# Two chained recurrent layers of 1024 steps: a third tile of layer 0 split for 88 columns, and the matmuls, rests and copies of a step put in another order

## What is computed

```python
def _L0_cond_ref(x, h0, Wx, Wh, b):
    xW = jnp.einsum('ntd,dh->nth', x, Wx) + b
    def step(h_prev, xw_t):
        h_next = jnp.tanh(h_prev @ Wh + xw_t)
        return (h_next, h_next)
    _, hs = jax.lax.scan(step, h0, jnp.swapaxes(xW, 0, 1))
    return jnp.swapaxes(hs, 0, 1)
...
    x = x + _L0_cond_ref(x, cond_1024, L0_cond_Wx, L0_cond_Wh, L0_cond_b)
    x = x + _L1_cond_ref(x, cond_1024, L1_cond_Wx, L1_cond_Wh, L1_cond_b)
```

## Time and profile before

| what | value |
|---|---|
| median of 3 runs | 2058.94 us (2058.87 to 2059.46) |
| the profiled execution | 2059.2 us, its span 2057.4 us |
| TensorE matmuls busy | 2046.2 us (99%) |
| TensorE weight loads busy | 1952.7 us (95%) |
| VectorE busy | 1837.9 us (89%) |
| ScalarE busy | 1539.9 us (75%) |
| GpSimd busy | 444.0 us (22%) |
| granted TensorE clock | full in all of 40 slices |

### The profile page before, as it was taken

How to read it: one execution, slowest core, us unless ns; L and a number is a source line. 1 busy time by engine, 2 the same in 40 slices (tenths; PEclk the granted TensorE clock), 3 DMA queues, 4 the chain that set the end, 5 groups by cost and what they waited for, 6 DMA issues and landing times.

```text
span 2057.4 us, 224159 instructions
## 1 busy us (share of the span) xinstructions
PE 2046.2 (99%) x98384; PEld 1952.7 (95%) x98384; DVE 1837.9 (89%) x12254; ACT 1539.9 (75%) x7426; POOL 444.0 (22%) x2054
## 2 busy tenths in 40 slices
PE   8999999999999999999999999999999999999999
PEld 7999999999999999999999999999999999999998
DVE  5999999999999999999999999999999999999997
ACT  5777777777777777777777777777777777777776
POOL 3222222222222222222222222222222222222221
PEclk9999999999999999999999999999999999999999
DMA  3000000000000000000000000000000000000000
GB/s 106 28 24 28 24 27 25 26 25 26 26 25 26 25 27 24 28 24 28 24 28 24 28 24 28 24 28 24 28 24 28 24 28 24 28 24 27 25 26 18
DMA packets 111995, 56.59 MB, mean 28 GB/s; under 512 B 12432, under 2 KB 111008, under 8 KB 111520
## 3 DMA queue, kind: packets, MB, share of 16 engines
q1 hardware_dynamic: 111168, 53.53, 9.0%
q10 hardware_dynamic: 576, 1.18, 0.2%
q0 software_dynamic: 32, 0.02, 0.0%
HBM read 37.90 MB, written 16.78 MB: 27 GB/s over the span
## 4 chain that ended last, share of the span: by engine, by line
PE 99%; DMA 1%; issue 0%; DVE 0%; ACT 0%; ACTq 0%; SPq 0%
PE ps_rec L303 44%; PE ps_rec L324 33%; PE ps_xw L279 22%; DMA wx<-wx_in 0%; DMA wh<-wh_in 0%; PE ps_rec L376 0%; DVE zt L541 0%; ACT h L445 0%; SPq L255 0%; ACTq L498 0%; ACTq L497 0%; DVE x_out L581 0%; DVE z L550 0%; SPq L254 0%
## 5 line engine op out<-in xcount | busy, mean ns | idle before, releaser
L303 PE MATMUL ps_rec<-wh,h 128*32 128x128 f32 x33024 | 1271.8, 273 | 4.1 <-ACT h L445 2.7
L445 ACT ACTIVATE h<-z 128x16 f32<-128x16 f32 x4066 | 709.2, 217 | 481.7 <-DVE z L550 475.4
L324 PE MATMUL ps_rec<-wh_part,h 128*32 128x128 bf16 x48792 | 1047.4, 219 | 1.5 <-issue 1.5
L303 PEld LDWEIGHTS ps_rec<-wh,h 128*32 128x32 f32 x33024 | 832.5, 109 | 79.6 <-ACT h L445 9.2
L324 PEld LDWEIGHTS ps_rec<-wh_part,h 128*32 128x32 bf16 x48792 | 890.1, 97 | 15.4 <-issue 1.9
L541 DVE STREAM_TRANSPOSE zt<-ps_rec 128x64 f32<-128x64 f32 x4096 | 778.8, 228 | 94.0 <-PE ps_rec L303 14.2
L214 POOL TENSOR_TENSOR h<-h 128x16 f32<-128x16 f32 x2032 | 430.1, 212 | 1589.4 <-DVE h L214 1589.4
L434 ACT ACTIVATE ps_rec<-xw,mask 128x128 f32<-128x128 f32 x2040 | 731.9, 359 | 9.5 <-issue 1.0
L550 DVE TENSOR_REDUCE z<-zt 128x16 f32<-128x48 f32 x4066 | 650.6, 199 | 0.9
L214 DVE TENSOR_TENSOR h<-h 128x16 f32<-128x16 f32 x2034 | 357.3, 176 | 110.7 <-ACT h L445 2.8
L279 PE MATMUL ps_xw<-wx,x_pe 128*32 128x128 f32 x8248 | 409.9, 273 | 0.5 <-issue 0.5
(11 more groups left out here) (23 smaller groups left out, 22.3 us busy)
## 6 DMA issues: line engine op xcount, KB each, us to landing
x_pe<-x_t SPq DMA_DIRECT2D x256, 64.0 KB, 1.9
x_dve<-x_t SPq DMA_DIRECT2D x256, 64.0 KB, 2.0
out_t<-x_out SPq DMA_DIRECT2D x256, 64.0 KB, 1.7
wh<-wh_in SPq DMA_DIRECT2D x1, 1024.0 KB, 5.2
wx<-wx_in SPq DMA_DIRECT2D x1, 1024.0 KB, 8.2
wx<-wx_in ACTq DMA_DIRECT2D x1, 512.0 KB, 5.0
wx<-wx_in SPq DMA_DIRECT2D x1, 512.0 KB, 4.8
wh<-wh_in SPq DMA_DIRECT2D x1, 512.0 KB, 7.9
```

The costliest lines, as they stand in the source:

```text
L303: mm = pe.matmul(rows(ps_rec[l][n % 2], g), h_step(l, n - 1)[:, k, :], wh[l][:, k, g * P:(g + 1) * P], start=False, stop=k == KC - 1 and n ...
L324: mm = pe.matmul(ps_rec[l][n % 2][32 * g:32 * g + 32, cols], h_bits(l, n - 1)[:, k, :], wh_part[l][:, i, to + cols.start:to + cols.stop], ...
L445: act.activation(h_of(l, n)[:, tiles, :], src[:, tiles, :], ACT.Tanh).then_inc(h_count(l, n)[0], 1)
```

## The change

Layer 0 gets its third tile (k = 2) in parts too, but for columns 0 to 87 of each group of 128 (`PART_COLS`). Columns 88 to 127 of this tile stay in one float32 matmul for each group, which holds only the 8 columns of the state as weights and writes block 0; the sums of layer 0's second half therefore begin at block 0. GpSimd makes a fifth set of parts at the start.

A slot becomes a `head` (layer 0's parts, both projected tiles, layer 1's whole tile 2) and a `tail` (layer 1's whole tile 3 and parts, layer 0's whole tiles of the next step). The hardware loop begins with a tail, so the wait for `s_wpart[0]` stands amid layer 1's whole tiles. `PROJECT` is regrouped in pairs.

For layer 0 VectorE makes both rests of tiles 0 and 1, one after the other, and GpSimd both of tile 2. For layer 1 GpSimd makes both rests. On ScalarE `pass_xm`, layer 0's copy and its seed go between tanh of layer 0 and `begin` of layer 1, in slots 0, 1 and 2 of four. `LOWEST` has one step of four that begins at block 1, where it had two.

```diff
-KB = (2, 2)
+KB = (3, 2)
...
-SIDE = P // 2
+PART_COLS = ((P, P, 88, 0), (P, P, 0, 0))
...
-PROJECT = (((0, 3), (1, 0)), ((1, 1), (1, 2)), ((1, 3), (0, 0)), ((0, 1), (0, 2)))
-
-
-BLOCKS = ((0, 1, 2), (1, 0, 2), (2, 1, 3), (3, 1, 2))
-LOWEST = (0, 0, 1, 1)
+PROJECT = ((0, (2, 3)), (1, (0, 1)), (1, (2, 3)), (0, (0, 1)))
+
+
+BLOCKS = ((0, 1, 2), (1, 0, 2), (2, 0, 1), (3, 1, 2))
+LOWEST = (0, 0, 0, 1)
...
-        def rest(eng, l, n, part, tiles):
+        def rest(eng, l, n, part, tiles=HALVES[0]):
...
+            def in_parts(l, n, k):
+
+                return 0 if is_whole(l, n) else PART_COLS[l][k]
+
+            def recur_whole(l, n, only=range(KC)):
 
 
                 if (l, n) == (0, 0):
                     pe.wait_ge(s_hinit, 2)
                     pe.wait_ge(begun[0], 1)
+                tiles = [k for k in range(KC) if in_parts(l, n, k) < P]
+                for k in only:
+                    if k not in tiles:
+                        continue
+                    cols = slice(in_parts(l, n, k), P)
                     if (l, n) == (0, 0):
                         if k % 2 == 0:
                             pe.wait_ge(s_wh0[k // 2], DMA)
                     elif k % 2 == 0 or k == tiles[0]:
                         pe.wait_ge(*h_count(l, n - 1, k // 2))
                     for g in range(QG):
+                        out, state = rows(ps_rec[l][n % 2], g)[:, cols], h_step(l, n - 1)[:, k, :]
+                        if cols.start:
+                            out, state = out[0:B, :], h_of(l, n - 1)[:, k, :]
+                        mm = pe.matmul(out, state, wh[l][:, k, g * P:(g + 1) * P][:, cols], start=False,
+                                       stop=k == KC - 1 and is_whole(l, n), skip_group_check=True,
                                        tile_position=(0, 32 * g))
+                if is_whole(l, n) and only[-1] == KC - 1:
+                    mm.then_inc(rec_done[l], 1)
 
             def recur_parts(l, n):
 
 
+                if is_whole(l, n):
                     return
+                for k in range(KB[l]):
+                    cols = slice(0, PART_COLS[l][k])
+                    if k % 2 == 0:
+                        pe.wait_ge(*split_count(l, n - 1, k // 2))
                     for i in range(PARTS):
                         for g in range(QG):
+                            at = k * D + g * P
+                            mm = pe.matmul(rows(ps_rec[l][n % 2], g)[:, cols], h_bits(l, n - 1)[:, k, :],
+                                           wh_part[l][:, i, at:at + P][:, cols], start=False,
+                                           stop=k == KB[l] - 1 and i == PARTS - 1, skip_group_check=True,
                                            tile_position=(0, 32 * g))
+                mm.then_inc(rec_done[l], 1)
+
+            def projection(s):
+
+                l, tiles = PROJECT[s % S4]
                 c = (s - S4) // S4 if l else (s + 6) // S4
                 if 0 <= c < NG or l == 0 and s < T:
+                    if tiles[0] == 0 and l == 0:
                         if c == 2:
                             pe.wait_ge(s_seed, 4)
                         else:
                             pe.wait_ge(seed0_done, 1)
+                    if tiles[0] == 0 and (l, c) == (1, 0):
                         pe.wait_ge(s_wx1, DMA)
+                    if tiles[0] == 0 and l == 1:
                         pe.wait_ge(xm_done, 1)
+                    for k in tiles:
+                        project(l, c, k)
+
+            def head(s):
 
                 if s < T:
                     recur_parts(0, s)
                 if s == 0:
                     pe.wait_ge(x_first[1], DMA)
+                    for k in (0, 1):
                         project(0, 1, k)
+                projection(s)
                 if (n := number(1, s)) is not None:
                     if n == 0:
                         pe.wait_ge(s_wh1, DMA)
                         pe.wait_ge(s_wpart[1], PARTS * KB[1])
+                    recur_whole(1, n, range(KC - 1))
+
+            def tail(s):
+
+                if (n := number(1, s)) is not None:
+                    recur_whole(1, n, range(KC - 1, KC))
                     recur_parts(1, n)
                     if T + LAG - S4 <= s < T + LAG - 1:
                         warm(ps_rec[0][0], IDLE)
+                if s + 1 < T:
                     recur_whole(0, s + 1)
 
...
-            for s in range(PARTED):
-                slot(s)
+            for s in range(PARTED - 1):
+                head(s)
+                tail(s)
+            head(PARTED - 1)
             pe.wait_ge(s_wpart[0], PARTS * KB[0])
             with pe.Fori(0, (T - PARTED) // RING, 1):
-                for s in range(PARTED, PARTED + RING):
-                    slot(s)
+                for s in range(PARTED - 1, PARTED - 1 + RING):
+                    tail(s)
+                    head(s + 1)
+            tail(T - 1)
             for s in range(T, T + LAG):
-                slot(s)
+                head(s)
+                tail(s)
...
+                if t == 0 and 0 <= r - 1 < NG:
+                    pass_xm(r - 1)
+                if t == 1 and 2 <= r + 1 < NG:
+                    copy(0, r + 1)
...
+                if t == 2 and 2 <= (c := r + 2) < NG + 2:
+                    if c < NG:
+                        act.wait_ge(x_pe_loaded, DMA * (c - 1))
...
+            for l, k in ((0, 0), (0, 1), (1, 0), (1, 1), (0, 2)):
...
-                    first = SPLITS[l] if (l, n) == (0, PARTED - 1) else 0
-                    if SPLITS[l] == 2:
-                        pool.wait_ge(*h_count(l, n))
-                        rest(pool, l, n, 1, LATE[l]).then_inc(late_done[l], 1)
-                    pool.wait_ge(rest_done[l], n + 1 if l else n + 2 - PARTED)
-                    rest(pool, l, n, 2, HALVES[0]).then_inc(split_count(l, n, 0)[0], 1 + first)
-                    if SPLITS[l] == 2:
-                        pool.wait_ge(late_done[l], n + 1 if l else n + 2 - PARTED)
-                        rest(pool, l, n, 2, LATE[l]).then_inc(split_count(l, n, 1)[0], 1)
+                    mine, done = (rest_done[1], n + 1) if l else (late_done, n + 2 - PARTED)
+                    tiles = HALVES[0] if l else slice(2, 3)
+                    pool.wait_ge(*h_count(l, n, 1 - l))
+                    rest(pool, l, n, 1, tiles).then_inc(mine, 1)
+                    pool.wait_ge(mine, done)
+                    rest(pool, l, n, 2, tiles).then_inc(split_count(l, n, 1 - l)[0], PAIR if (l, n) == (0, PARTED - 1) else 1)
...
-                at = LOWEST[n % S4] * B
                 for i, tiles in enumerate(HALVES):
+                    at = LOWEST[n % S4] * B
+                    end = at + PARTS * B
+                    if l == 0 and i:
+                        at = 0
                     dve.wait_ge(zt_done[l], piece_count(n, i))
                     dve.tensor_reduce(z[l][n % 2][:, :].rearrange("p (k b) -> p k b", k=KC)[:, tiles, :],
                                       zt[l][n % 2][:, :].rearrange("p (k r) -> p k r", r=ROWS)[
-                                          :, tiles, at:at + PARTS * B].rearrange("p k (i b) -> p k b i", b=B),
+                                          :, tiles, at:end].rearrange("p k (i b) -> p k b i", b=B),
...
-            def rest_first(l, n):
-                if is_split(l, n):
-                    dve.wait_ge(*h_count(l, n, 0))
-                    rest(dve, l, n, 1, HALVES[0]).then_inc(rest_done[l], 1)
+            def rests(n):
+                if is_split(0, n):
+                    dve.wait_ge(*h_count(0, n, 0))
+                    rest(dve, 0, n, 1).then_inc(rest_done[0], 1)
+                    dve.wait_ge(rest_done[0], n + 2 - PARTED)
+                    rest(dve, 0, n, 2).then_inc(split_count(0, n, 0)[0], PAIR if n == PARTED - 1 else 1)
...
-                    rest_first(0, n0)
+                    rests(n0)
...
-                if n1 is not None:
-                    rest_first(1, n1)
```

121 lines of the change are left out of this document (28 added, 93 removed).

## The result

The changed kernel takes 2075.22 us, the median of 4 runs (2073.70 to 2077.47), where the kernel before takes 2058.90 in the same session: a ratio of 1.0081, with a 95% interval of 1.0064 to 1.0099. It is slower by 0.8%; the prediction was 2033 us, outside its range of 2028 to 2060. The profiled execution took 2077.47 us, its span 2074.5, against 2059.2 and 2057.4 before.

The account below looks back on a forecast made before the run. TensorE's stream of matmuls was taken as the bound. From 2059.2 us, 1016 steps x (1.9805 - 1.953) = 27.9 us saved and 1.4 lost at the start gave 2033 us, range 2028 to 2060.

Parts of the forecast that it names:

- a stream of matmuls: On TensorE: the loop's length is what its matmuls take, 1.9805 us for one step of both layers.
- loop of latencies: Layer 1's chain from parts through sums and tanh to the next whole tile's load: 1.948 us, nearly tied with the stream.
- The period of the stream: TensorE's step with layer 0's third tile in parts: 1.9805 - 0.2186 + 0.189 = 1.951 us.
- The law of columns: TensorE matmul groups: 0.416 ns a column plus 2.4 ns a group; 117 ns for the parts, 72 ns for the float32 group.
- GpSimd's pair of rests: Layer 1's two rests on GpSimd: -0.04 to +0.013 us on the period, taken as no cost; other end 1.964 us.
- ScalarE's full gap: Copy, seed and begin between ScalarE's tanhs fill the gap, not over: nothing, other end 20 ns in one step of four.
- a tie that jitters: Stream and layer 1's loop tie within 3 ns, so 2 ns were added to the period, making 1.953 us.
- the fourth block of a sum: Layer 0's sum in one step of four: 17 ns of VectorE at most, against 30 ns of slack.
- B: Rival: short matmuls have a floor, in the 40-column float32 group; 100 ns or more makes it slower, 2070 us; chance 0.12.
- C: Rival: loading weights, not columns, holds a bf16 group at 55.7 ns; period 2.001, 2081 us; chance 0.05.
- A: Rival: the rest path or ScalarE's fuller gap becomes the bound, period 1.965 to 1.978, 2044 to 2058 us; chance 0.08.
- D: Rival: the change doesn't do what it says, since latency already holds the period; 2059 to 2061 us; chance 0.05.

Follow-up runs that it names:

- run 2: The kernel before with only its loop edge moved amid layer 1's whole tiles, against the kernel before: 2092.57 us, ratio 1.0166.
- run 8: The changed kernel with the loop's edge moved behind both of layer 1's whole tiles, ahead of its parts: 2036.34 us, ratio 0.9895.
- run 7: The changed kernel with its edge ahead of both of layer 1's whole tiles and two start-up waits taken out of the body: 2037.30 us, ratio 0.9898.
- run 1: The changed kernel with the loop's edge put back between two slots, ahead of layer 0's parts: 2074.37 us, ratio 1.0076.
- runs 5 and 13: The changed kernel with its edge ahead of layer 1's whole tiles, one step later: 2073.01 us; the same shifted 8 instructions by extra warm-up: 2073.95 us.
- run 9: The changed kernel with a loop body of eight steps instead of four, so 127 edges instead of 254: 2060.62 us, ratio 1.0011.
- run 10: The changed kernel with the edge behind both of layer 1's whole tiles, but without layer 0's third tile in parts: 2065.50 us, ratio 1.0035.
- run 12: The changed kernel with the edge behind both of layer 1's whole tiles, and 64 instead of 88 columns in parts: 2050.80 us, ratio 0.9961.
- run 11: The changed kernel with the edge behind both of layer 1's whole tiles, and all 128 columns of the third tile in parts: 2056.95 us, ratio 0.9996.
- run 4: The changed kernel with the edge one tile earlier, between the projection and both of layer 1's whole tiles: 2058.48 us, ratio 1.0002.

## Why the prediction was wrong

**The step that failed** is one that the prediction doesn't have. In "the change part by part" the loop that begins amid layer 1's whole tiles is not costed at all. In the part on the start, the prediction priced only the wait for the split weights, which comes earlier with the loop, and the longer first pass. So the edge stood in the sum at nothing, without a reason; it costs 0.162 us at each of 254 edges, 41 us, which is more than the 28 us saved. Under "What bounds the kernel now" the loop is "a stream of matmuls": the branch at its end was in the trace of before, and I had not read it. Weight loads of before, between layer 0's whole tiles and parts, without an edge and at one:

```profile
1001.29 0.41 PEld L303 LDWEIGHTS ps_rec<-wh,h 128*32 128x32 f32 x16
1001.68 0.45 PEld L324 LDWEIGHTS ps_rec<-wh_part,h 128*32 128x32 bf16 x24
...
1003.27 0.41 PEld L303 LDWEIGHTS ps_rec<-wh,h 128*32 128x32 f32 x16
1003.70 0.41 PEld L324 LDWEIGHTS ps_rec<-wh_part,h 128*32 128x32 bf16 x24
```

At the edge the bf16 loads follow the whole tiles' by 0.43 where at 1001.29 to 1001.68 they follow by 0.39: the branch between them had delayed these by 0.04, and two whole tiles (0.437) covered it. One can tell a cover that thin from nothing only by asking what stands between the two.

**The rule that the runs give.** TensorE's queue can run ahead of the matmuls only from the last wait that ended just in time. From that release to the branch it takes 0.12 us with 8 loads between, 0.17 to 0.18 with 16. From branch to the next load it takes 0.263. The cover is the matmuls queued since the release, plus any time by which the release came ahead of its due. What the sum has over the cover is lost at each edge:
- after, amid the whole tiles: 0.12 + 0.263 = 0.383; one whole tile covers 0.219: 0.164, measured 0.162.
- run 2, the same with the 0.03 by which h comes early in the kernel before: 0.134, measured 0.134.
- before and run 8, behind both: 0.44 against 0.437, and before has the 0.03 on top: next to nothing. Measured: nothing in before, and the edge's step 0.003 longer in run 8. That 0.003 needn't be the branch's: run 7, with its branch elsewhere, has it too, in layer 0's whole tiles (0.293 for 0.290), behind the four-block sum.
- run 1, behind layer 0's whole tiles, which are one tile and 40 columns now (0.29 us): 0.44 - 0.29 = 0.15, measured 0.159.

The figures are fitted to these runs. The expectation of run 8 was written with the same reasoning before it ran. The rule says nothing of the second hole of runs 5 and 13.

So the third tile took the cover of the old place away (run 1), the new place has too little of its own (run 2), and either alone would have eaten the gain. The "loop of latencies" of the prediction makes layer 1's h come just in time, so at this edge the queue has no other lead. That the edge is the cause is shown by run 2 (it alone costs 34 us), by runs 7 and 8 (moved, it costs nothing) and by run 9 (half as many cost half). What takes the 0.263 isn't: the branch's own record has 0.207 of it.

The Trainium skill, "Runtime: NRT & Kernel Launch", section "Instruction fetch mechanics", says that a taken branch whose target isn't in the current window of two pages stalls until the target page is fetched. The trace agrees in kind, 0.263 us at each of the edges; no run here shows whether a fetch is what it consists of, and the page has no figure for it.

The same skill, "Advanced Engine Details and Errata", section "Control Flow Timing", gives compare-and-branch as about 108 ns. Here the record is 207 to 208 ns in every kernel at the edges from 500 to 1500 us, and 263 pass until work goes on; the measurement decides.

**What held.** The period of the stream: 1.951 in every step without an edge, to the nanosecond the sum 1.9805 - 0.2186 + 0.189. The law of columns under 128: 88-column groups start 38 to 39 ns apart, the float32 group takes 71 ns. The two tied loops of layer 1: its loads at 1001.71 and 1002.15 have their matmuls 0.02 us behind, just due. GpSimd's pair of rests takes 0.50, so the second starts 0.29 after the first, 0.21 and my upper 0.08: the load (1002.15) comes 0.05 after it ends (1002.10), just in time, and the period isn't 1.964. ScalarE's full gap cost nothing that the steps show.

The start: the stall stands where I put it, near 24, released by GpSimd, 1.53 us for 1.4.

```profile
22.91 0.40 PE L279 MATMUL ps_rec<-wh,h 128*32 128x128 f32 x8
24.84 0.43 PE L279 MATMUL ps_rec<-wh,h 128*32 128x128 f32 x8 [1.53 <-POOL wh_part L505]
28.18 0.52 PE L279 MATMUL ps_rec<-wh,h 128*32 128x128 f32 x10 [1.20 <-issue]
31.91 0.40 PE L297 MATMUL ps_rec<-wh_part,h 128*32 128x128 bf16 x15 [1.00 <-issue]
35.64 0.46 PE L279 MATMUL ps_rec<-wh,h 128*8 128x40 f32 x11 [1.31 <-issue]
```

The three gaps of the first pass are 3.5 us together for 2.4 in the earlier trace rows: the "nothing to 0.5 us" was too small for this kernel. In run 8 the stall is 1.75 us, but only two gaps are left, 2.0 us together, and step 20 begins at 52.01: there the start costs nothing more than before.

**Two terms that were mis-sized.** The 2 ns for "a tie that jitters" is 5 to 6 ns: mean less middle value is 0.0064 in after and about 0.008 in run 8, for 0.003 before. That is most of why run 8 gives 2036.3 and not 2033. Why the steps jitter more isn't shown. And the fourth block of a sum takes 55 ns (0.264 for 0.209) where the prediction had 17 at most; it costs 6 us in run 10 and 4 in run 12, and next to nothing with 88 columns.

**The rivals.** B and C need a longer period of every step, and none has it: the 40-column group takes 71 ns where B needs 100, and bf16 groups shrink with their columns where C has them at 55.7. The floor of 25 ns that the prediction cites from the Trainium skill did not show for single passes: rounds of two passes came 35.5 ns apart, so 17.8 for each. A shows in run 11 alone, at 128 columns. D falls with run 8. None of the four named the edge. The signs that I had listed would have misled too: "TensorE busy all through" and "one stall near 24" both hold in the slower kernel, and a period from the engines' counts gives the mean, 1.998, which the list puts down to B or C. Only the distances sorted by place in the body show that three steps of four are right.

## What to carry to other kernels

A loop's edge is an instruction sequence with a duration, and it stands in the queue of the engine that the kernel is bound by: put it behind the longest run of work that needs no just-in-time wait, and cost it anew whenever that run is shortened or the edge is moved. Read a saturated engine by the distance of starts, sorted by place in the loop's body, never by its busy share. Keep start-up waits out of the body, for they are executed in each pass.

## What the runs showed of the hardware that I had not expected

- From TensorE's branch to the first load of the body 0.263 us pass, the same in six kernels (0.27 to 0.28 in some where the edge is hidden, as in run 8); at 254 edges that is 67 us of which queued matmuls can hide all (run 8, 2036 us) or little (after, 2075 us).
- Instructions just behind an edge can come late by 0.12 to 0.15 us more, and a shift of the body by 16 or 24 TensorE instructions takes that away, 2073.0 to 2038.6 and 2039.3, while 8 leaves it at 2074.0 and moves the hole four loads nearer to the body's start. So it belongs to one place in memory. Why that place is slow is open: only three shifts were run.
- From the end of tanh to the load that waits for it 0.113 us pass where the wait is an instruction of its own (run 4), and 0.051 where the load carries it (run 7).
- A sum over four blocks of PSUM's turned rows takes VectorE 0.264 us where one over three takes 0.209.
- GpSimd sees its own result 0.08 us after it, VectorE 0.03: the pair at 1001.60 takes 0.50, which is two times 0.21 and 0.08; VectorE's in the earlier trace rows took 0.38 for two times 0.176.
